# Value loads for two steps at a time, and a value ring that is released and filled by halves, in a graph-attention kernel

## The chip, the cores and the metric

The kernel runs on one core of a Trainium2 chip. The metric is the device time of one launch in microseconds (us). Before the change it is 1956.38 us, the median of three runs (1952.86 to 1957.16).

## What is computed

One graph-attention layer with four heads over 8192 nodes, followed by a residual and a layer norm. Cut to what matters:

```python
Wh = (x @ W.T).reshape(n, 4, 32)                      # n = 8192
score_l, score_r = einsum(Wh, a_l), einsum(Wh, a_r)   # n x 4 each
e = score_l[:, :, None] + score_r.T[None]             # e[n, h, m]
e = where(e >= 0, e, 0.2 * e)                         # leaky relu
e = where((adj + eye > 0)[:, None, :], e, -inf)
out = einsum('nhm,mhd->nhd', softmax(e, axis=2), Wh)  # over m
x = layernorm(x + elu(out))
```

The exponential of a leaky relu has two branches, each of which is a product of a factor of the row and a factor of the column. So the kernel never forms the softmax's matrix. For each node it sums the columns' weighted values twice, over the neighbours with e >= 0 and over the others, and gives each sum its row factor at the end. The two sums are matmuls of 0/1 masks with a table of values.

## The kernel before

**Tiling.** Rows (destination nodes) go in NC = 8 chunks of 1024 (eight sub-tiles of 128), heads in NP = 2 pairs, columns (source nodes) in 32 steps of two tiles of 128. A pass is one chunk c with one pair of heads p; there are 16 passes of 32 steps, 512 steps in all, counted by q. In the text "step 276" is the one with q = 276, and a place in a pass is s = q % 32.

**One step.** ScalarE makes two or three and VectorE one or two of the four 128x1024 comparisons of the step (`bmask`, lines 446 and 591). VectorE ANDs them with the adjacency (`mask_b`, line 603) and XORs the result with the adjacency for the other branch (`mask_c`, line 609). TensorE does 32 matmuls with `bmask`, in some steps turns one pair of adjacency tiles (`turn_pair`, line 315, 16 matmuls), and does 32 matmuls with `cmask` (line 335). ScalarE copies a turned pair from PSUM to `acache` (line 414). `bmask` has four slots and `cmask` two. From step 32 on a pair is turned in every even step.

**Queues.** Every engine's program is written out by hand. SyncE issues every DMA: 396 values per tile and partition from the table `v_scratch` in DRAM into `vring`, the adjacency into the two buffers `abuf` (`load_block`, line 177, 2 MB in two DMAs per four turned tiles), the rows' scores `lrow` (line 186, 1 MB, once a pass), and once a chunk the finished output and the residual's input (`store_y` line 216, `load_xr` line 211, four DMAs of 128 KB each). SyncE takes them strictly in order, so a DMA whose semaphore wait is not met holds up all behind it.

**The ring of values.** `vring` has four slots, one for each step, and `load_v(q)` (line 194) fills slot q % 4. It waits for `mm_done` of q - 3, that is until TensorE has ended step q - 4. The loop issues `load_v(q + 3)` in iteration q, so a load goes out when step q - 1 ends. TensorE waits for `v_in[slot]` at the head of each step.

**Order around the change.** Iteration q of SyncE's loop issues, in this order: the value load, an adjacency block if one is due (in the steady part every fourth iteration, q % 4 == 3), `lrow` at s = 3, and output and residual input at s = 16. The passes of the chunks 1 to 6 are in a hardware loop on TensorE (`pe.Fori(1, NC - 1)`); its program jumps back at the steps 128, 192, 256, 320 and 384.

Of the kernel before, what the change touches and what calls it, by code (L numbers as in the profile page):

```python
# [6 lines left out]
def gat_kernel(nc, x, adj, W, a_l, a_r, out):  # L7
# [10 lines left out]
    NP = 2  # L18
    HP = H // NP
    STEPS = NT // 2  # L20
    Q = NC * NP * STEPS
# [46 lines left out]
    with ctx:  # L68
        def sb(name, shape, dt):
            return ctx.enter_context(nc.sbuf_tensor(name, shape, dt))  # L70

        def sem(name):
            return ctx.enter_context(nc.semaphore(name))

        l_dram = nc.dram_tensor("l_scratch", [NC, H * SUB, P], fp32, kind="Internal").ap()
        v_dram = nc.dram_tensor("v_scratch", [NP, P, NT, VW], bf16, kind="Internal").ap()
# [6 lines left out]
        vring = sb("vring", [P, 4, 2, VW], bf16)  # L83
# [63 lines left out]

        a_loaded = [sem("a_loaded0"), sem("a_loaded1")]
        tr_done, evac_done, pack_made, diag_done = sem("tr_done"), sem("evac_done"), sem("pack_made"), sem("diag_done")
        v_in = [sem(f"v_in{k}") for k in range(4)]  # L150
        lrow_in, cmp_act, cmp_dve = [sem("lrow_in0"), sem("lrow_in1")], sem("cmp_act"), sem("cmp_dve")
        b_ready, c_ready, half_done, mm_done, bank_free = (sem(s) for s in ("b_ready", "c_ready", "half_done", "mm_done", "bank_free"))
        dn_step, w_ready, pool_step, mn_ready, em_ready = (sem(s) for s in ("dn_step", "w_ready", "pool_step", "mn_ready", "em_ready"))
# [5 lines left out]
        def wait(eng, s, value):  # L159

            if not (isinstance(value, int) and value <= 0):
                eng.wait_ge(s, value)
# [8 lines left out]
        def _(sp):  # L171
            def load_block(n):
                c, jb = n // BLOCKS, n % BLOCKS
                wait(sp, tr_done, JB // 2 * (n - 1))
                for half in range(2):
                    rows = adj[c * CI + half * CI // 2:c * CI + (half + 1) * CI // 2, jb * JB * P:(jb + 1) * JB * P]
                    sp.dma_start(abuf[:, n % 2, half * SUB // 2:(half + 1) * SUB // 2],
                                 rows.rearrange("(j p) m -> p j m", p=P)).then_inc(a_loaded[n % 2], 16)

            def load_lrow(c, p):  # L180

                if c > 0:
                    sp.wait_ge(cmp_act, step_no(c - 1, p, STEPS - 1) + 1)
                    sp.wait_ge(cmp_dve, step_no(c - 1, p, STEPS - 1) + 1)
                src = l_dram[c:c + 1, p * HP * SUB:(p + 1) * HP * SUB].rearrange("o i n -> o (i n)").to_broadcast([P, HP * CI])
                sp.dma_start(lrow[:, p].rearrange("q h n -> q (h n)"), src).then_inc(lrow_in[p], 16)

            def load_v(q):
                c, p, s = WHERE[q]
                wait(sp, mm_done, q - 3)  # L190
                if c == 0 and s % EVERY_STEPS == 0:
                    n = p * NG + s // EVERY_STEPS
                    sp.wait_ge(v_out[n % VS], 16 * (n // VS + 1))
                sp.dma_start(vring[:, q % 4], v_dram[p, :, 2 * s:2 * s + 2]).then_inc(v_in[q % 4], 16)

            def store_v(n):

                p, g = n // NG, n % NG
                sp.wait_ge(v_lo, n + 1)
                sp.dma_start(v_dram[p, :, G * g:G * g + G], vt[:, n % VS].rearrange("q t i e -> q t (i e)")).then_inc(v_out[n % VS], 16)  # L200
# [12 lines left out]
            def store_y(c):  # L213
                sp.wait_ge(y_ready, c + 1)
                for s in range(4):
                    sp.dma_start(as_bytes(out, c, s), yout[s::4]).then_inc(y_stored, 16)
# [14 lines left out]
            for g in range(NG):  # L231
                if g in (1, 3, 5, 7):
                    load_block({1: 2, 3: 3, 5: 4, 7: 5}[g])
                store_v(g)
            for q in range(3):
                load_v(q)

            loaded, turned = 6, AHEAD
            for q in range(Q):
                c, p, s = WHERE[q]  # L240
                if q + 3 < Q:
                    load_v(q + 3)
                while loaded < NC * BLOCKS and JB // 2 * (loaded - 1) <= turned:
                    load_block(loaded)
                    loaded += 1
                turned += len(TURNED[q])
                if s == 3 and p == 1 and c < NC - 1:
                    load_lrow(c + 1, 0)
                if s == 3 and p == 0 and c > 0:
                    load_lrow(c, 1)  # L250
                if q < STEPS + 1 and s % EVERY_STEPS == 0 and q > 0:
                    store_v(NG + q // EVERY_STEPS - 1)
                if s == 16 and p == (0 if c else 1):
                    if c > 0:
                        store_y(c - 1)
                    load_xr(c)
# [6 lines left out]
        def _(pe):  # L263
            def settle():
                pe.sem_inc(passed, 1)
# [52 lines left out]
            def step(c, p, u, k, first=False, turned=None):  # L318

                slot, cslot = k % 4, k % 2  # L320
                q = (c * NP + p) * STEPS + 8 * u + k
                w = c * NP + p

                def opens(bank):
                    wait(pe, bank_free, BANKS * (w - 1) + bank + 1)
                    if not isinstance(c, int):
                        settle()

                def product(mask, item, i, h, b, j):
                    bank, at = item // PB, item % PB  # L330
                    opening = first and i == 0 and at == 0
                    if opening:
                        opens(bank)
                    col = (h * 2 + b) * S3
                    return nc.tensor.matmul(psum[:, bank, at * S3:(at + 1) * S3], mask[:, i, j * P:(j + 1) * P],  # L335
                                            vring[:, slot, i, col:col + S3], start=opening, stop=True, skip_group_check=True)

                pe.wait_ge(v_in[slot], 16 * ((c * NP + p) * (STEPS // 4) + 2 * u + k // 4 + 1))
                pe.wait_ge(b_ready, q + 1)
                if not isinstance(q, int):  # L340
                    settle()
                for i in range(2):
                    for h in range(HP):
                        for j in range(SUB):
                            last = product(bmask[:, slot, h], h * SUB + j, i, h, 0, j)
                last.then_inc(half_done, 1)
                if turned:
                    turn_pair(*turned)
                pe.wait_ge(c_ready, q + 1)
                if not isinstance(q, int):  # L350
                    settle()
                for i in range(2):
                    for h in range(HP):
                        for j in range(SUB):
                            last = product(cmask[:, cslot, h], (HP + h) * SUB + j, i, h, 1, j)
                last.then_inc(mm_done, 1)
# [428 lines left out]
```

## Time and profile before

| what | value |
|---|---|
| median of three runs | 1956.38 us |
| the profiled execution | 1956.05 us |
| its span, first to last instruction | 1954.3 us |
| TensorE busy | 1676.7 us (86%) |
| VectorE busy | 1850.1 us (95%) |
| ScalarE busy | 1696.2 us (87%) |
| mean granted TensorE clock | 0.946 |
| value loads | 512 of 198 KB, median 3.4 us from issue to landing |
| adjacency loads | 256 of 1 MB, median 8.0 us |

The matmuls of the steps start from 91 us to 1927 us. The three compute engines are all nearly full, so the busy shares alone do not say which one sets the pace in a stretch; that is read from the waits and from the timeline. Landings of DMAs are read from the DMA view of a window that holds one issue.

### The profile page before, as it was taken

Reading aid. Unit: us, or ns where it says so; the run is one execution under the profiler, and the core shown is the slowest. Engines: PE = TensorE matmul, PEld = TensorE weight load, DVE = VectorE, ACT = ScalarE, POOL = GpSimd, SP = SyncE. Lnnn points to the kernel's source line nnn. Section 1 sums busy time; section 2 is a strip of 40 time slices with the busy share of each in tenths; the row PEclk is TensorE's granted clock in tenths of the full one; section 3 lists DMA queues with packets and bytes.
Section 4 is the critical chain, followed back from the end, with each engine's and each line's share of the span. In section 5 each row is a group of like instructions: output and inputs, shape, how many; then the busy total and the mean of one; then the engine's idle time right before and its main releaser. Section 6 shows DMA issues by size and latency. Waiting matters only on the chain.

```text
span 1954.3 us, 83257 instructions
## 1 busy us (share of the span) xinstructions
PE 1676.7 (86%) x37063; PEld 1650.0 (84%) x37063; DVE 1850.1 (95%) x2056; ACT 1696.2 (87%) x1791; POOL 228.2 (12%) x106
## 2 busy tenths in 40 slices
PE   5188899798978999788988989889898889989894
PEld 5187799797978989788988989789897889989894
DVE  6699999999999999999999999999999999999995
ACT  3599899798988999798989989789897899979892
POOL 1000100401022010211004010220102110040103
PEclk8599999999999999999999999899998999999997
DMA  7899576676666767666766767567675657665221
GB/s 230 313 328 341 194 257 225 202 228 229 209 200 218 255 210 238 202 212 211 236 220 207 236 220 232 193 205 255 207 236 181 227 190 255 230 200 170 60 68 28
DMA packets 240287, 418.06 MB, mean 214 GB/s; under 512 B 14400, under 2 KB 104896, under 8 KB 238016
## 3 DMA queue, kind: packets, MB, share of 16 engines
q1 hardware_dynamic: 240064, 414.83, 64.6%
q8 instruction: 171, 2.80, 0.6%
q14 instruction: 52, 0.43, 0.1%
HBM read 397.48 MB, written 17.30 MB: 212 GB/s over the span
## 4 chain that ended last, share of the span: by engine, by line
ACT 44%; DVE 22%; PE 18%; issue 9%; DMA 5%; POOL 1%; SPq 0%; DVEq 0%; ACTq 0%; POOLq 0%
ACT bmask L446 40%; PE psum L335 15%; DVE bmask L591 7%; DVE bmask L603 5%; DVE cmask L609 5%; ACT acache L414 3%; DMA abuf<-in_adj_dram 3%; DVE acc L615 2%; DMA vring<-v_scratch 2%; PE trp L315 1%; PE psum L280 1%; DMA v_scratch<-vt 1%; DVE st L657 1%; PE psum L289 0%; DVE acache L539 0%
## 5 line engine op out<-in xcount | busy, mean ns | idle before, releaser
L446 ACT ACTIVATE bmask<-lrow,rtab 128x1024 fp8e4<-128x1024 f32 x1450 | 1540.7, 1149 | 11.5 <-PE psum L335 11.5
L335 PE MATMUL psum<-vring,bmask 128*128 128x99 bf16 x16384 | 843.0, 210 | 96.1 <-DVE bmask L603 48.1
L335 PE MATMUL psum<-vring,cmask 128*128 128x99 bf16 x16384 | 844.6, 211 | 89.1 <-DVE cmask L609 80.4
L335 PEld LDWEIGHTS psum<-vring,bmask 128*128 128x128 fp8e4 x16384 | 780.5, 99 | 107.8 <-issue 99.0
L335 PEld LDWEIGHTS psum<-vring,cmask 128*128 128x128 fp8e4 x16384 | 778.5, 99 | 100.5 <-issue 83.4
L603 DVE TENSOR_TENSOR bmask<-bmask,acache 128x1024 int32<-128x1024 int32 x512 | 632.2, 1235 | 41.3 <-ACT bmask L446 32.3
L609 DVE TENSOR_TENSOR cmask<-acache,bmask 128x1024 int32<-128x1024 int32 x512 | 654.7, 1279 | 11.8 <-PE psum L335 11.7
L591 DVE TENSOR_SCALAR bmask<-lrow,rtab 128x1024 fp8e4<-128x1024 f32 x598 | 500.0, 848 | 0.0
L414 ACT CAST acache<-trp 128x512 int32<-128x512 f32 x256 | 148.5, 580 | 167.3 <-PE trp L315 167.0
L720 POOL TENSOR_TENSOR late<-acc,wgt 128x1024 f32<-128x1024 f32 x16 | 45.0, 2810 | 1493.8 <-DVE wgt L645 1493.8
L315 PE MATMUL trp<-pack,abuf 128*128 128x32 bf16 x4096 | 144.1, 177 | 53.7 <-ACT acache L414 32.0
L315 PEld LDWEIGHTS trp<-pack,abuf 128*128 128x128 bf16 x4096 | 128.4, 97 | 56.1 <-issue 32.8
L615 DVE TENSOR_REDUCE acc<-psum 128x165 f32<-128x495 f32 (+1 forms) x112 | 62.7, 621 | 0.8 <-PE psum L335 0.8
L729 POOL TENSOR_SCALAR late<-late 128x512 f32<-128x512 f32 x16 | 36.6, 2289 | 1.4
L419 ACT CAST vt<-acache 128x1056 bf16<-128x1056 f32 x16 | 17.1, 1101 | 17.4 <-DMA v_scratch<-vt 15.8
L743 POOL TENSOR_TENSOR vrs<-mv,epsc 128x8 f32<-128x8 f32 x8 | 7.8, 980 | 191.3 <-DVE mv L661 191.3
L745 POOL TENSOR_TENSOR vrs<-vrs,epsc 128x8 f32<-128x8 f32 x8 | 27.4, 3422 | 0.6
L402 ACT COPY acache<-psum 128x280 f32<-128x280 f32 x32 | 11.0, 395 | 17.9 <-PE psum L280 17.9
L726 POOL TENSOR_TENSOR late<-late 128x512 f32<-128x512 f32 x16 | 25.2, 1576 | 1.3
L453 ACT ACTIVATE late<-late 128x512 f32<-128x512 f32 x16 | 9.9, 617 | 17.4 <-POOL late L729 17.4
L746 POOL TENSOR_TENSOR late<-late,mv 128x1024 f32<-128x1024 f32 x8 | 23.3, 2911 | 0.0
L500 DVE COPY bmask<-psum 128x512 f32<-128x512 f32 x16 | 11.1, 692 | 11.1 <-PE psum L289 11.0
(60 smaller groups left out, 258.5 us busy)
## 6 DMA issues: line engine op xcount, KB each, us to landing
abuf<-in_adj_dram SPq DMA_DIRECT2D x256, 1024.0 KB, 8.0
vring<-v_scratch SPq DMA_DIRECT2D x512, 198.0 KB, 3.4
lrow<-l_scratch SPq DMA_DIRECT2D x16, 1024.0 KB, 10.8
v_scratch<-vt SPq DMA_DIRECT2D x16, 792.0 KB, 9.5
bmask<-in_x_dram SPq DMA_DIRECT2D x16, 256.0 KB, 2.9
late<-in_x_dram SPq DMA_DIRECT2D x32, 128.0 KB, 4.8
out_dram<-late SPq DMA_DIRECT2D x32, 128.0 KB, 6.1
l_scratch<-cmask SPq DMA_DIRECT2D x1, 128.0 KB, 3.7
```

Of the source, the lines that this page charges most:

```text
L315: last = nc.tensor.matmul(trp[:, i, j * P // 4:(j + 1) * P // 4], block_hi, pack[:, :], start=True, stop=True)
L335: return nc.tensor.matmul(psum[:, bank, at * S3:(at + 1) * S3], mask[:, i, j * P:(j + 1) * P], vring[:, slot, i, col:col + S3], start=open ...
L414: nc.scalar.copy(acache[:, at:at + 2].rearrange("p t n -> p (t n)").bitcast(i32), trp.rearrange("p i n -> p (i n)")).then_inc(evac_done, 1)
L446: last = nc.scalar.activation(bmask[:, q % 4, h, i], lrow[:, p, h], ACT.Relu, bias=rtab[:, t, H + hh:H + hh + 1], scale=BIG, saturate=False)
L591: last = nc.vector.tensor_scalar(bmask[:, q % 4, h, i], lrow[:, p, h], rtab[:, t, hh:hh + 1], None, ALU.is_ge, saturate=False)
L603: nc.vector.tensor_tensor(m, m, adj_words(c, s), ALU.bitwise_and).then_inc(b_ready, 1)
L609: nc.vector.tensor_tensor(mask_words(cmask[:, q % 2]), adj_words(c, s), mask_words(bmask[:, q % 4]), ALU.bitwise_xor).then_inc(c_ready, 1)
L615: nc.vector.tensor_reduce(acc[:, b * PB:b * PB + n], psum[:, b, 0:n * S3].rearrange("p (i s e) -> p i e s", s=3, e=E), AX.X, ALU.add).then ...
L720: nc.gpsimd.tensor_tensor(pm[:, :], acc[:, :, 0:DK], wgt.rearrange("p (i o) -> p i o", o=1).to_broadcast([P, ITEMS, DK]), ALU.mult).then_i ...
L726: nc.gpsimd.tensor_tensor(ov[:, :, mine].rearrange("p j (h d) -> p h j d", h=HP), p2[:, 0], p2[:, 1], ALU.add).then_inc(pool_step, 1)
L729: nc.gpsimd.tensor_scalar(mn[:, :, mine], ov[:, :, mine], 0.0, None, ALU.min).then_inc(mn_ready, 1)
L745: nc.gpsimd.tensor_tensor(vrs[:, :], vrs[:, :], epsc[:, SUB:2 * SUB], ALU.pow).then_inc(pool_step, 1)
```

## The change

One DMA now brings the values of two steps (396 KB instead of 198 KB). The four slots are two halves. A load fills a half and waits until both steps that used it are done. `v_in` has two semaphores instead of four; both steps of a half wait for the same value. SyncE issues a load in every odd iteration only.

```diff
-        v_in = [sem(f"v_in{k}") for k in range(4)]
+        v_in = [sem("v_in0"), sem("v_in1")]
...
             def load_v(q):
+
                 c, p, s = WHERE[q]
-                wait(sp, mm_done, q - 3)
+                half = q // 2 % 2
+                wait(sp, mm_done, q - 2)
...
-                sp.dma_start(vring[:, q % 4], v_dram[p, :, 2 * s:2 * s + 2]).then_inc(v_in[q % 4], 16)
+                sp.dma_start(vring[:, 2 * half:2 * half + 2].rearrange("p s i e -> p (s i) e"),
+                             v_dram[p, :, 2 * s:2 * s + 4]).then_inc(v_in[half], 16)
...
-            for q in range(3):
+            for q in (0, 2):
                 load_v(q)
...
-                if q + 3 < Q:
+                if q % 2 == 1 and q + 3 < Q:
                     load_v(q + 3)
...
-                pe.wait_ge(v_in[slot], 16 * ((c * NP + p) * (STEPS // 4) + 2 * u + k // 4 + 1))
+                pe.wait_ge(v_in[slot // 2], 16 * ((c * NP + p) * (STEPS // 4) + 2 * u + k // 4 + 1))
```

On SyncE, around the chunk's output and residual input (s = 16), the kernel before has these rows (`abuf` is adjacency, `vring` values, `out_dram` the output, `late<-in_x_dram` the residual's input):

```order
L194 DMA vring<-v_scratch 128x792 [waits mm_done] x4
L177 DMA abuf<-in_adj_dram 128x4x512 [waits tr_done]
L177 DMA abuf<-in_adj_dram 128x4x512
L194 DMA vring<-v_scratch 128x792 [waits mm_done]
L216 DMA out_dram<-late 32x8x128 [waits y_ready]
L216 DMA out_dram<-late 32x8x128 x3
L211 DMA late<-in_x_dram 32x8x128 [waits y_ready]
L211 DMA late<-in_x_dram 32x8x128 x3
L194 DMA vring<-v_scratch 128x792 [waits mm_done] x3
```

At the same place the changed kernel has these:

```order
L196 DMA vring<-v_scratch 128x1584 [waits mm_done] x2
L177 DMA abuf<-in_adj_dram 128x4x512 [waits tr_done]
L177 DMA abuf<-in_adj_dram 128x4x512
L219 DMA out_dram<-late 32x8x128 [waits y_ready]
L219 DMA out_dram<-late 32x8x128 x3
L214 DMA late<-in_x_dram 32x8x128 [waits y_ready]
L214 DMA late<-in_x_dram 32x8x128 x3
L196 DMA vring<-v_scratch 128x1584 [waits mm_done] x2
```

Four value loads between two adjacency blocks became two. The value load that stood between the adjacency block and the output is now ahead of the block, as the second half of a pair.

Where `lrow` is loaded (s = 3), SyncE before has:

```order
L194 DMA vring<-v_scratch 128x792 [waits mm_done] x4
L177 DMA abuf<-in_adj_dram 128x4x512 [waits tr_done]
L177 DMA abuf<-in_adj_dram 128x4x512
L186 DMA lrow<-l_scratch 128x2048 [waits cmp_dve,cmp_act]
L194 DMA vring<-v_scratch 128x792 [waits mm_done] x4
```

and now:

```order
L196 DMA vring<-v_scratch 128x1584 [waits mm_done] x2
L177 DMA abuf<-in_adj_dram 128x4x512 [waits tr_done]
L177 DMA abuf<-in_adj_dram 128x4x512
L186 DMA lrow<-l_scratch 128x2048 [waits cmp_dve,cmp_act]
L196 DMA vring<-v_scratch 128x1584 [waits mm_done] x2
```

The block and `lrow` stand behind the same iteration's value load as before, and that load's wait is now for one step more.

## Rows read from the trace of the kernel before

**Rows 1.** Page, costliest groups: count, busy us, mean ns, idle before and releaser.
```profile
L446 ACT ACTIVATE bmask<-lrow,rtab 128x1024 fp8e4<-128x1024 f32 x1450 | 1540.7, 1149 | 11.5 <-PE psum L335 11.5
...
L414 ACT CAST acache<-trp 128x512 int32<-128x512 f32 x256 | 148.5, 580 | 167.3 <-PE trp L315 167.0
```
**Rows 2.** Waits: who waited for whom, us in total, times, longest.
```profile
ACT acache L414 <- PE trp L315: 167.0, 73, 8.6
...
PE psum L335 <- DMA vring<-v_scratch: 18.5, 5, 16.9
```
**Rows 3.** Windows: us, busy PE, PEld, DVE, ACT, POOL (instructions), clock, DMA share.
```profile
862.50:895.00 32.50, 32.46 (x769) 32.34 (x766) 31.97 (x34) 32.50 (x35) 0.00 (x0) 1.00 0.78 249
```
**Rows 4.** Timeline of SyncE's queue, 960 to 977 us: start, us, what.
```profile
961.89 2.15 SPq L177 DMA_DIRECT2D abuf<-in_adj_dram  x2
964.39 9.74 SPq L194 DMA_DIRECT2D vring<-v_scratch  x4
```
**Rows 5.** DMA issues in the window 964.3:964.6, last number us to landing.
```profile
vring<-v_scratch SPq DMA_DIRECT2D x1, 198.0 KB, 8.1
```
**Rows 6.** Timeline of TensorE, start of step 244.
```profile
976.48 1.59 PE L335 MATMUL psum<-vring,bmask 128*128 128x99 bf16 x32
```
**Rows 7.** Timeline of SyncE's queue, 1077 to 1099 us.
```profile
1081.11 0.98 SPq L177 DMA_DIRECT2D abuf<-in_adj_dram  x2
1083.61 0.34 SPq L194 DMA_DIRECT2D vring<-v_scratch  x1
1083.99 3.19 SPq L216 DMA_DIRECT2D out_dram<-late  x4
...
1091.21 2.14 SPq L194 DMA_DIRECT2D vring<-v_scratch  x3
```
**Rows 8.** DMA issues in the window 1091.15:1091.5, the load of step 276.
```profile
vring<-v_scratch SPq DMA_DIRECT2D x1, 198.0 KB, 3.8
```
**Rows 9.** Timeline of TensorE, step 276: its start and its turned pair.
```profile
1095.71 1.59 PE L335 MATMUL psum<-vring,bmask 128*128 128x99 bf16 x32
1097.13 0.56 PE L315 MATMUL trp<-pack,abuf 128*128 128x32 bf16 x16
```
**Rows 10.** Timeline of ScalarE: it takes the pair turned in step 276.
```profile
1098.43 0.58 ACT L414 CAST acache<-trp 128x512 int32<-128x512 f32 x1
```
**Rows 11.** DMA totals of the windows 1085:1087 (2048-byte packets) and 1090.4:1092.4 (512-byte).
```profile
DMA packets 380, 0.75 MB, mean 374 GB/s; under 512 B 15, under 2 KB 15, under 8 KB 380
...
DMA packets 1349, 0.66 MB, mean 330 GB/s; under 512 B 82, under 2 KB 1348, under 8 KB 1349
```
**Rows 12.** Timeline of SyncE's queue, 920 to 940 us.
```profile
921.38 2.35 SPq L177 DMA_DIRECT2D abuf<-in_adj_dram  x2
924.13 0.34 SPq L186 DMA_DIRECT2D lrow<-l_scratch  x1
925.40 10.57 SPq L194 DMA_DIRECT2D vring<-v_scratch  x4
```
**Rows 13.** DMA issues in the window 925.3:925.6, the load of step 231.
```profile
vring<-v_scratch SPq DMA_DIRECT2D x1, 198.0 KB, 9.3
```
**Rows 14.** Timeline of TensorE, start of step 232.
```profile
938.32 1.59 PE L335 MATMUL psum<-vring,bmask 128*128 128x99 bf16 x32
```
**Rows 15.** Timeline of TensorE, two idle times of about 2.6 us.
```profile
142.75 0.59 PE L315 MATMUL trp<-pack,abuf 128*128 128x32 bf16 x16 [2.63 <-DMA abuf<-in_adj_dram]
...
693.69 1.60 PE L335 MATMUL psum<-vring,cmask 128*128 128x99 bf16 x32 [2.55 <-DVE cmask L609]
```
**Rows 16.** Windows just after these two idle times; the third number from the end is the clock.
```profile
142.50:145.80 3.30, 3.04 (x48) 3.08 (x49) 2.80 (x3) 2.42 (x3) 0.00 (x0) 0.50 0.99 343
...
693.80:697.00 3.20, 3.03 (x64) 2.80 (x62) 3.20 (x4) 2.76 (x4) 1.10 (x1) 1.00 0.19 45
```
**Rows 17.** Page, DMA queues: packets, MB, share of 16 engines.
```profile
q8 instruction: 171, 2.80, 0.6%
```
**Rows 18.** Timeline of TensorE at the jump back of its loop, step 256.
```profile
1020.83 2.83 PE L335 MATMUL psum<-vring,bmask 128*128 128x99 bf16 x32 [6.69 <-DVE bmask L603]
```

## The prediction

> **What bounds the kernel now.** I read the costliest groups first, then the waits, and then the timeline and the DMA view of a few narrow windows.
>
> The groups give the pace. ScalarE's comparisons and its copies of turned pairs add up to 1540.7 + 148.5 = 1689 us over 512 steps, 3.30 us a step [rows 1]. The steps take 3.6 us on average (91 to 1927 us). ScalarE is idle for 167 us in front of the copy, waiting for TensorE's turned pair [rows 1, 2]. So ScalarE sets the pace wherever TensorE has kept up, and where TensorE is late ScalarE waits for it. In an undisturbed stretch both are full: in 32.5 us ScalarE is busy for 32.50 us and TensorE for 32.46 us [rows 3]. TensorE's lateness of a microsecond or two is therefore not free. It reaches ScalarE as soon as the turned pair comes later than ScalarE gets to it.
>
> The change touches what TensorE waits for at the head of a step. Before, this wait is nearly nothing: 18.5 us in all, 16.9 of them once, before the first step [rows 2]. The reader is to see how little room there is behind that small number.
>
> **What the change does to a load.** Before, the load of step q is issued when step q - 4 ends, with three whole steps to land in. Now the pair (q, q + 1) is issued when step q - 3 ends, and its first step has only two. The adjacency block stands behind a value load in SyncE's queue, so its issue too comes one step later than before. In the steady part the queue is now pair, pair, block. The first pair after a block goes out two steps after it and lands behind it. All of these share one queue, and what I need is how long that queue takes to drain, counted from the block's issue.
>
> *An ordinary place (step 244).* The block is issued at 961.89 and the load of step 243 at 964.39 [rows 4], landing 8.1 us later at 972.5 [rows 5], which is 10.6 us behind the block's issue. The load of 964.39 went out when step 239 ended. Now the pair goes out at that time and the block 0.38 us later (1083.99 - 1083.61, what SyncE needs from one value load to the next DMA [rows 7]), at 964.77. The same bytes and one step's values more are then in the queue. The 198 KB take 0.5 us at 374 GB/s [rows 11]. The pair lands at 964.77 + 10.6 + 0.5 = 975.9. TensorE starts step 244 at 976.48 [rows 6]. It fits with 0.6 us to spare. This is one of the tight ones, since TensorE runs at full pace here. Some ninety places are of this kind and I count them at nothing. At worst, with 0.5 us more in the queue, a few of them are late by tenths.
>
> *Output and residual input (s = 16, p = 0, chunks 1 to 7: seven places, step 276 is one).* Behind the block there is another 1 MB in 512-byte packets. The block is issued at 1081.11 [rows 7] and the load of step 276 lands at 1091.21 + 3.8 = 1095.0 [rows 7, 8], 13.9 us later. TensorE starts step 276 at 1095.71 [rows 9], so before there are 0.7 us to spare. Now the block goes out at 1083.61 + 0.38 = 1083.99. The bytes ahead of the pair are those ahead of the old load, less one step's values that went out earlier. The pair's second step puts them back. So it lands at 1083.99 + 13.9 = 1097.9, and TensorE stands for 2.2 us. The bounds: if SyncE and not the queue sets the landing, its eight issues end 7.2 us after they start [rows 7], at about 1092.2, and with 3.8 + 0.5 us the pair is late by 0.8 us. With 0.5 us more in the queue it is 2.7 us. The DMA engines moved 330 GB/s right before the load's landing [rows 11], so the queue was full and I take 2.2.
>
> How much of this reaches ScalarE? The pair of adjacency tiles turned in step 276 is ready at 1097.13 + 0.56 = 1097.69 [rows 9], and ScalarE, busy until then, takes it at 1098.43 [rows 10]. It hides 0.7 us. 1.5 us are left, times 7 = 10 us (bounds 0 to 14).
>
> *lrow (s = 3, 14 places, step 232 is one).* The block goes out at 921.38, lrow at 924.13, the load of step 231 at 925.40 [rows 12]. That load lands 9.3 us later at 934.7 [rows 13], 13.3 behind the block. Now the block goes out at 925.40 + 0.38 = 925.8, and the pair (232, 233) lands at 925.8 + 13.3 + 0.5 = 939.6. TensorE starts step 232 at 938.32 [rows 14], so it is late by 1.3 us. With ScalarE's 0.7 us hidden 0.6 are left. In the seven places with p = 0, VectorE has the previous chunk's lines 652 and 657 in its queue one and two steps later and is itself the laggard there, so I count nothing. In the seven with p = 1 it is 0.6 x 7 = 4 us. Bounds for all: 0 to 14 x 1.3 = 18 us.
>
> *The clock.* An idle TensorE can be granted 1.2 GHz instead of 2.4 afterwards. Of two idle times of about the same length, one of 2.63 us was followed by a granted clock of 0.50 for 3.3 us, and one of 2.55 us was not (1.00) [rows 15, 16]. The seven stands of 2.2 us are just of this size. A block of 32 matmuls takes 2.83 us at the low clock [rows 18] and 1.60 at the high one [rows 15], and in 3.3 us TensorE falls about 1.4 us behind. ScalarE's slack is by then used up. Half of seven is 3.5 x 1.4 = 5 us (0 to 10).
>
> *The loop's jumps.* At five steps TensorE's program jumps back, and it stands for 6.69 us in the one shown [rows 18]. Programs are read by DMA on a queue of their own, 171 packets of 16 KB in the span [rows 17], on the same DMA engines. The block used to be issued one step before this jump and is now issued at the jump, so such a read meets another load. If it gets ahead of the block, up to all of it could go: 5 x 6.69 = 33 us. If it comes behind the whole block, whose queue takes 10.6 us, it is 5 x (10.6 - 6.7) = 20 us worse. The row nearest is the one of today, with the block already in the queue, so I take a small gain of 0.6 us each, 3 us.
>
> *The first step.* It now waits for 396 KB instead of 198, 0.5 us. SyncE issues 256 DMAs fewer, at 0.32 us each, but it waits for TensorE nearly always; nothing. TensorE has as many waits as before.
>
> *The packets.* They double from 1584 to 3168 bytes. From 512 to 2048 bytes the rate rises from 330 to 374 GB/s, 13% for a factor of four [rows 11]. A pair takes 1.1 us, so even the whole 13% is 0.14 us. Nothing in the sum.
>
> The Trainium skill ("Perfetto Trace Analysis", DMA Optimizations) holds that batching small transfers, for example from 2 KB to 4 or 8 KB, can improve throughput dramatically when a kernel is bound by DMA. By that rule the pairs would land much earlier, the late places would go and the crowded first 24 steps would get faster. The two rates of rows 11 do not bear a dramatic step out in this range of sizes.
>
> **The sum.** 10 + 4 + 5 - 3 + 0.5 = 16.5 us, on the profiled execution's own 1956.05 us (span 1954.3 and 1.75 around it), 0.3 under the median. The forecast is 1972 us. The adjacency blocks have one step less too, but they need not land before the turn four steps later, some 14 us after their issue against about 10 us of queue.
>
> **The rivals.**
>
> 1. *Everything lands on the path, and more: 1997 us.* No slack in ScalarE, every late place counted whole: 7 x 2.2 + 14 x 1.3 = 34 us, with the low clock at each of the seven, 10 us, less 3 for the jumps. For it speaks that ScalarE is never idle in the 32.5 us of rows 3. Against it speaks the slack of rows 10.
>
> 2. *The late pairs are hidden: 1956 us.* The queue drains faster since no single value loads stand in it, or TensorE's start in these places is late for other reasons. It needs landings 2 us earlier at the seven places. Against it speak the full DMA engines.
>
> 3. *Faster, by the jumps: 1943 us.* The place is the head of a pass, steps 128 to 384. The program's read finds an empty queue since the block is issued behind it. It decides from about 17 us on, half of the 33: the price is 1956 + 20 (without my 3) - 33 = 1943. For it speaks that the block is today in the queue when the jump comes and will not be. Against it: the block follows 0.4 us after the jump.
>
> 4. *Batching pays: 1966 us.* With packets a fixed 13% cheaper, a pair is 0.14 us earlier. At 21 places this is 3 us, and the first 24 steps gain 12 pairs x 0.14 = 2 us. It changes the size and not the sign. The page's rule named above is this rival; so far as the rows go it is worth 5 us and no more.
>
> **How the numbers follow.** The forecast with its own range 1962 to 1984 has 0.66, the fourth rival 0.04 within it, rival 1 0.12, rival 2 0.10, rival 3 0.08. Faster by over 0.2% (4 us, about what a measurement of this kernel can tell from no change) comes from rival 3: 0.08. No change is rival 2: 0.10. Slower has the rest, 0.82. The range 1957 to 1990 leaves out rival 3, most of rival 2 and the worst of rival 1.
>
> **What the profile of the changed kernel would show.** In the waits, TensorE's wait for `vring` grows from 18.5 us to 40 to 60 us, in about 21 pieces besides the first, at s = 20 of the passes with p = 0 (about 2 us each) and at s = 8 of nearly all (about 1 us each). ScalarE's 167 us for the turned pair grow by 12 to 20 us. A landing of a pair two steps behind a block takes 4 to 5 us, and 7 to 8 us with lrow or the output in the queue. Idle before step 256 a little under 6.7 us. The prediction is wrong if these pieces are there and the time is not longer, if the pairs at s = 20 land before TensorE comes, or if the gaps at the jumps change by more than 2 us each.

## The result, and the profile after

The changed kernel takes 1992.9 us, median of four runs (1987.91 to 1997.71), against 1956.77 us. The ratio is 1.0189, with a 95% interval of 1.016 to 1.0217. Repeated in a later call it is 1.0194 (1.0163 to 1.0224). The change costs about 37 us. The direction was the forecast one, and the size was more than twice the forecast's 16.5 us and outside its range. Single runs of the kernel before spread from 1938.6 to 1968.5 us over all calls (three slow runs of 3.3 to 8.3 ms, one each of three kernels, are left out of all ratios), so a place in one trace is read to a microsecond only where a mechanism stands behind it.

The page's first part and the lines that answer to [rows 1], of the changed kernel (its lines stand three further down than before):

```profile
span 1991.8 us, 83001 instructions
...
PE 1692.0 (85%) x37063; PEld 1665.0 (84%) x37063; DVE 1850.4 (93%) x2056; ACT 1699.1 (85%) x1791; POOL 227.5 (11%) x106
...
L449 ACT ACTIVATE bmask<-lrow,rtab 128x1024 fp8e4<-128x1024 f32 x1450 | 1539.0, 1144 | 13.7 <-PE psum L338 13.7
...
L417 ACT CAST acache<-trp 128x512 int32<-128x512 f32 x256 | 148.2, 579 | 199.1 <-PE trp L318 198.8
```

No engine has more instructions to do. TensorE's busy time grew all the same, from 1676.7 to 1692.0 us, for its 37063 matmuls, as its mean granted clock went from 0.946 to 0.941. ScalarE's work is the same to 2 us, and its idle time in front of the copy of a turned pair has grown from 167 to 199 us. The 32 us are most of the 37.5 us between the two spans: ScalarE waits for a TensorE that is late. Why TensorE is late is in the waits of the changed kernel (us in total, times, longest), where [rows 2] has 18.5 us for the values:

```profile
PE psum L338 <- DMA vring<-v_scratch: 45.4, 19, 16.4
PE psum L338 <- DVE acc L618: 38.6, 40, 4.0
...
PE psum L338 <- issue: 27.6, 31, 3.4
PE trp L318 <- issue: 19.9, 6, 5.1
```

The wait for values grew by 27 us. The last two lines are idle times of TensorE that no semaphore explains; together they were 19.2 us before and are 47.5 us now. Part of this growth is a name only: 21.6 us of the 47.5 stand at the loop's five jumps, and there the kernel before has about 32 us of idle time that the trace puts down to VectorE ([rows 18] is one of the five). Elsewhere this idle time grew from 19 to 26 us.

**Behind the output (step 276).** The changed kernel's timeline of SyncE's queue and of TensorE, and the landing of the pair (DMA issues, window 1120.2:1120.6), to be set beside [rows 7 to 9]:

```profile
1110.15 0.34 SPq L196 DMA_DIRECT2D vring<-v_scratch  x1
1110.53 1.48 SPq L177 DMA_DIRECT2D abuf<-in_adj_dram  x2
1112.05 3.45 SPq L219 DMA_DIRECT2D out_dram<-late  x4
1115.55 4.69 SPq L214 DMA_DIRECT2D late<-in_x_dram  x4
1120.28 0.60 SPq L196 DMA_DIRECT2D vring<-v_scratch  x1
```

```profile
vring<-v_scratch SPq DMA_DIRECT2D x1, 396.0 KB, 4.2
```

```profile
1120.80 1.60 PE L338 MATMUL psum<-vring,cmask 128*128 128x99 bf16 x32
1124.71 1.59 PE L338 MATMUL psum<-vring,bmask 128*128 128x99 bf16 x32 [2.31 <-DMA vring<-v_scratch]
1126.14 0.56 PE L318 MATMUL trp<-pack,abuf 128*128 128x32 bf16 x16
```

The pair lands at 1120.28 + 4.2 = 1124.5, which is 13.95 us behind the block's issue. The forecast had 13.9, and an idle time of 2.2 us; it is 2.31. SyncE needs 8.2 us for the eight issues, so the pair goes out about 4 us after its release (step 273 ended at about 1116.3). In ScalarE's timeline the turned pair now has to be waited for:

```profile
1126.73 0.59 ACT L417 CAST acache<-trp 128x512 int32<-128x512 f32 x1 [1.68 <-PE trp L318]
```

1.68 us against the forecast's 1.5. The same idle time of 1.7 to 2.8 us stands at all seven such places.

**Behind lrow (step 232).** In the changed kernel TensorE waits 1.19 us for the pair, against the 1.3 forecast from [rows 12 to 14]:

```profile
964.05 1.59 PE L338 MATMUL psum<-vring,bmask 128*128 128x99 bf16 x32 [1.19 <-DMA vring<-v_scratch]
```

Its twin at step 296 is put down to another releaser:

```profile
1196.82 1.59 PE L338 MATMUL psum<-vring,bmask 128*128 128x99 bf16 x32 [1.28 <-DVE bmask L606]
```

The pair and not VectorE was the last to come there: the block was issued at 1182.85 and the pair landed 13.7 us later, at 1196.5, just before TensorE started. So the sum of the vring line above is short by such places.

**At the jump (step 256).** The idle time of 6.69 us [rows 18] became two, and the second lies in the middle of the turned pair:

```profile
1043.33 2.15 PE L338 MATMUL psum<-vring,bmask 128*128 128x99 bf16 x32 [3.71 <-DVE acc L618]
...
1050.70 0.48 PE L318 MATMUL trp<-pack,abuf 128*128 128x32 bf16 x11 [5.09 <-issue]
...
1062.58 1.60 PE L338 MATMUL psum<-vring,cmask 128*128 128x99 bf16 x32 [0.80 <-DVE cmask L612]
```

The last line is TensorE's wait for VectorE in step 259. In the kernel before it is 1.8 us longer:

```profile
1036.80 2.83 PE L335 MATMUL psum<-vring,cmask 128*128 128x99 bf16 x32 [2.56 <-DVE cmask L609]
```

VectorE sets the pace at the head of a pass (it is busy for 15.10 of the 15.20 us from 1020.8 to 1036 in the kernel before), and TensorE's longer stand is hidden behind it. From step 252 to step 260 the kernel before takes 37.7 us and the changed one 36.8. Over all five jumps these eight steps take 187.6 us before and 185.5 us now (185.3 in the second trace of the changed kernel). So the jumps cost the changed kernel nothing: they give back 2 us.

**The clock.** After the late pair of step 276 the clock stayed at its upper level, and after the one of step 340 it was at the lower (windows; the third number from the end is the clock):

```profile
1124.70:1128.00 3.30, 3.29 (x81) 3.30 (x82) 2.99 (x4) 1.62 (x3) 0.00 (x0) 1.00 0.99 309
1358.40:1361.70 3.30, 3.30 (x54) 3.30 (x52) 3.17 (x5) 1.40 (x2) 0.00 (x0) 0.50 0.98 314
```

It fell at four of the seven places.

### The profile page after: what moved, and what is told of

It reads as the page before. It is cut to its first block, busy times and chain, and to the rows that moved or that the text cites. A ratio compares the mean times of both kernels' runs of the same rounds, so it can differ in the third digit from the quotient of the medians.

```text
span 1991.8 us, 83001 instructions
## 1 busy us (share of the span) xinstructions
PE 1692.0 (85%) x37063; PEld 1665.0 (84%) x37063; DVE 1850.4 (93%) x2056; ACT 1699.1 (85%) x1791; POOL 227.5 (11%) x106
## 4 chain that ended last, share of the span: by engine, by line
ACT 36%; PE 25%; DVE 19%; issue 9%; DMA 7%; SPq 2%; POOL 1%; DVEq 0%; ACTq 0%; POOLq 0%
ACT bmask L449 33%; PE psum L338 22%; DVE bmask L594 6%; DVE bmask L606 5%; DMA vring<-v_scratch 4%; DVE cmask L612 4%; ACT acache L417 2%; DMA abuf<-in_adj_dram 2%; PE trp L318 2%; DVE acc L618 2%; SPq L214 1%; DMA v_scratch<-vt 1%; PE psum L283 1%; SPq L219 1%; DVE st L660 1%
## 5 line engine op out<-in xcount | busy, mean ns | idle before, releaser
L449 ACT ACTIVATE bmask<-lrow,rtab 128x1024 fp8e4<-128x1024 f32 x1450 | 1539.0, 1144 | 13.7 <-PE psum L338 13.7
L338 PE MATMUL psum<-vring,bmask 128*128 128x99 bf16 x16384 | 851.8, 211 | 113.8 <-DMA vring<-v_scratch 45.4
L338 PEld LDWEIGHTS psum<-vring,bmask 128*128 128x128 fp8e4 x16384 | 788.4, 99 | 127.4 <-issue 117.9
L612 DVE TENSOR_TENSOR cmask<-acache,bmask 128x1024 int32<-128x1024 int32 x512 | 646.0, 1262 | 29.0 <-PE psum L338 28.4
L740 POOL TENSOR_TENSOR late<-late 128x1024 f32<-128x1024 f32 x8 | 22.7, 2840 | 0.6
```

Source lines behind the costliest of these rows:

```text
L449: last = nc.scalar.activation(bmask[:, q % 4, h, i], lrow[:, p, h], ACT.Relu, bias=rtab[:, t, H + hh:H + hh + 1], scale=BIG, saturate=False)
L612: nc.vector.tensor_tensor(mask_words(cmask[:, q % 2]), adj_words(c, s), mask_words(bmask[:, q % 4]), ALU.bitwise_xor).then_inc(c_ready, 1)
```

## The experiments

Theory A says that pairs of values land late behind a block with something else in the queue. Rival B says that the block's new time disturbs the reads of TensorE's program. Rival C says that the larger DMA is itself the cost. All ratios are against runs of the kernel before on the same chip; a difference of two ratios from different calls is one between two chips.

### Eight slots, all issue times kept

```diff
-        vring = sb("vring", [P, 4, 2, VW], bf16)
+        vring = sb("vring", [P, 8, 2, VW], bf16)
...
-                wait(sp, mm_done, q - 2)
+                wait(sp, mm_done, q - 4)
...
-                if q % 2 == 1 and q + 3 < Q:
-                    load_v(q + 3)
+                if q % 2 == 1 and q + 5 < Q:
+                    load_v(q + 5)
```

This is cut, and set against the changed kernel. `v_in` has four semaphores for the four halves, and `w_nat` and `w_t` lie in `acc` to make room.

> The changed kernel with eight slots (four halves): every DMA of SyncE goes out at the same time as in the changed kernel, but a pair of values is for two steps later, so its first step has four steps to land in and not two. w_nat and w_t share memory with acc. Theory A (pairs of values that land after TensorE has come, behind the adjacency block and lrow or the output): all these idle times go, about 34 us of the 36, and what is left is the start of the kernel, where blocks are waited for; 1959 to 1968 us, wait for vring only before the first step. Rival B (the blocks' later issue disturbs the reads of TensorE's program): nothing of that is changed here, so 1980 us or more.

Measured: 1.0065 (1.0041 to 1.009). The waits of this kernel:

```profile
PE psum L338 <- issue: 39.5, 34, 3.5
PE psum L338 <- DVE acc L618: 34.7, 40, 3.7
...
PE psum L338 <- DMA vring<-v_scratch: 16.3, 1, 16.3
PE trp L318 <- issue: 15.6, 7, 3.6
```

The wait for values is the one before the first step. Giving the pairs room takes 1.25% (24 us) off. What stays is 0.65%, more than the few microseconds of the start, and the idle time that no semaphore explains is 55 us, 21 of them at the five jumps. So theory A has two thirds of the loss, and something else has a third.

### Two single loads, released as the pair is

```diff
-                wait(sp, mm_done, q - 3)
+                wait(sp, mm_done, q - 2 - q % 2)
-                if q + 3 < Q:
+                if q % 2 == 1 and q + 3 < Q:
                     load_v(q + 3)
+                    load_v(q + 4)
```

> The kernel before, with its single loads of 198 KB and four semaphores, but both loads of a pair are issued together when the second of the two old steps has ended, as the changed kernel does. Theory A (the lateness of the release, not the size of the DMA): the same as the changed kernel within 5 us, 1988 to 1998 us; SyncE's second issue costs 0.3 us and the first step's values land 0.5 us earlier, so if anything 1 to 4 us less. Rival C (one DMA of 396 KB with 3168-byte packets is itself the cost): near the kernel before, 1956 to 1965 us.

Measured: 1.0269 (1.0231 to 1.0307), 0.8% worse than the pair. Rival C falls; the expectation of 1 to 4 us less was wrong in sign. SyncE's queue and TensorE at step 296, and that load's landing (window 1200.2:1200.3):

```profile
1193.71 0.80 SPq L194 DMA_DIRECT2D vring<-v_scratch  x2
1194.55 0.98 SPq L177 DMA_DIRECT2D abuf<-in_adj_dram  x2
1195.63 0.45 SPq L186 DMA_DIRECT2D lrow<-l_scratch  x1
1200.24 0.81 SPq L194 DMA_DIRECT2D vring<-v_scratch  x2
...
1209.03 1.15 PE L336 MATMUL psum<-vring,bmask 128*128 128x99 bf16 x22 [2.69 <-DMA vring<-v_scratch]
```

```profile
vring<-v_scratch SPq DMA_DIRECT2D x1, 198.0 KB, 8.5
```

The step's values land 14.2 us behind the block's issue (13.7 with the pair), and the block itself goes out 0.46 us later, because SyncE issues two loads before it. The idle time is 2.69 us where the pair has 1.28. With the release as it now is, one DMA is better than two. Why by 0.8% is open in part: of the 15 us between the two traces' spans 8 lie in steps 24 to 64, and no run looks into them.

### The block one step later in the kernel before

```diff
                 while loaded < NC * BLOCKS and JB // 2 * (loaded - 1) <= turned:
+                    if q > 32:
+                        wait(sp, mm_done, q + 1)
                     load_block(loaded)
```

> The kernel before with one thing more: from step 33 on SyncE issues an adjacency block only when the step of that iteration has ended, one step later, as in the changed kernel. Value loads behind it in SyncE's queue are then due at once and go out at nearly the same time as before. Theory A: nothing waits for the block, and value loads land up to 1 us later than before with up to 1 us of room; 1956 to 1964 us. Rival B (the block's new place disturbs the reads of TensorE's program): 1966 us or more, with more idle time in front of TensorE that no semaphore explains, at the jumps and inside the passes.

Measured: 1.0279 (1.024 to 1.0319). Its waits:

```profile
PE psum L337 <- DMA vring<-v_scratch: 75.6, 42, 16.2
...
PE trp L317 <- issue: 14.8, 5, 4.0
...
PE psum L337 <- issue: 13.8, 20, 1.9
```

The number would fit rival B, and the first line says otherwise; the unexplained idle time is 29 us, 9 more than before, and cannot hold 55 us. The load of step q % 4 == 3 goes out at its old time and now has the block directly in front of it, not one step earlier. Most of the loss is behind lrow: the 14 steps with s = 7 have 42 of the 59 us of waits behind the first one. At step 231, one of them, the block goes out at 951.26 and the load at 952.79, which lands 11.1 us later at 963.9, 12.6 us behind the block, and TensorE starts at 964.08. I had allowed it 1 us of lateness. The run tells of the queue and says little of program reads. It also suggests why the changed kernel does not lose more: its two values of a pair stand ahead of the block.

### lrow at s = 5

```diff
-                if s == 3 and p == 1 and c < NC - 1:
+                if s == 5 and p == 1 and c < NC - 1:
-                if s == 3 and p == 0 and c > 0:
+                if s == 5 and p == 0 and c > 0:
```

> The changed kernel with lrow issued at s = 5 of a pass and not at s = 3, so that no adjacency block is in front of it and no pair of values directly behind both. Theory A, as the profile after has it (the 14 late pairs at s = 8 pass on almost whole, 1.2 us each): 15 to 19 us less, 1974 to 1978 us, and the waits for vring at s = 8 are gone. The forecast's own reckoning (0.6 us at seven of them and nothing at the others): 4 us less, 1989 us.

Measured: 1.0192 (1.0157 to 1.0228), no gain. The late pairs at s = 8 are gone, and two steps later stands this (TensorE's timeline, step 234):

```profile
963.41 0.88 PE L338 MATMUL psum<-vring,bmask 128*128 128x99 bf16 x16
966.21 0.88 PE L338 MATMUL psum<-vring,bmask 128*128 128x99 bf16 x16 [1.91 <-issue]
```

In the DMA view of 962 to 967 us a program packet starts while the data queue is full:

```profile
q1 hardware_dynamic: 907, 1.89, 100.2%
q8 instruction: 1, 0.02, 1.1%
```

TensorE stops between two matmuls of one block of 32, where it waits for no semaphore. Theory A's 15 to 19 us less did not come; a gain of 4 us, the forecast's, would be within the noise. That moving 1 MB by two steps only changed what it was in the way of fits this place. But the unexplained idle time of the whole run, 50 us, is only 2 us above the changed kernel's, so a gain that was taken back is not shown.

### Output and residual input at s = 18

```diff
-                if s == 16 and p == (0 if c else 1):
+                if s == 18 and p == (0 if c else 1):
```

> The changed kernel with the output and the residual's input issued at s = 18 and not at s = 16, behind a pair of values two steps after the adjacency block and no longer directly behind the block. Theory A (late pairs at s = 20 pass on almost whole, with the low clock at about half of them; the profile after shows 19 us over s = 12 to 32 of the seven passes): 14 to 22 us less than the changed kernel if nothing else is hit, ratio to before about 1.009 to 1.012. Rival D (the same bytes hit something else there, as lrow did when it was moved, a read of TensorE's program): a ratio of 1.016 to 1.020.

Measured: 1.0089 (1.0057 to 1.0121), and in the next call but one 1.0106 (1.0076 to 1.0135). SyncE's queue and TensorE around step 276:

```profile
1094.48 0.98 SPq L177 DMA_DIRECT2D abuf<-in_adj_dram  x2
1100.25 0.34 SPq L196 DMA_DIRECT2D vring<-v_scratch  x1
1100.63 2.64 SPq L219 DMA_DIRECT2D out_dram<-late  x4
...
1106.19 1.59 PE L338 MATMUL psum<-vring,bmask 128*128 128x99 bf16 x32
```

The pair goes out 5.8 us behind the block, ahead of the output, and TensorE does not stand. Seven places are worth about 0.9%, 18 us. Theory A holds for them, and rival D falls.

### Eight slots, the block at its old time

```diff
-                if q % 2 == 1 and q + 5 < Q:
-                    load_v(q + 5)
+                if q % 2 == 0 and q + 4 < Q:
+                    load_v(q + 4)
...
+                    wait(sp, mm_done, q)
                     load_block(loaded)
```

> Merged loads alone: one DMA for two steps into eight slots, issued when step q - 1 of even iterations q ends, for the steps q + 4 and q + 5, so a pair has four steps to land in, and an adjacency block goes out when the same step ends as in the kernel before (one step earlier than in the changed kernel and in the run with eight slots). Theory A with the part of rival B that the first runs left (4 us of program reads at s = 10 come from the block's later issue): ratio to before 0.996 to 1.002, no waits for vring behind the first step, and idle time in front of TensorE at s = 10 of the passes with p = 1 back to about 0.5 us each. If merging itself costs (rival C), 1.005 or more.

Measured: 0.9983 (0.9959 to 1.0008), 0.8% less than the first run with eight slots. Its waits:

```profile
PE psum L339 <- issue: 20.3, 21, 6.0
...
PE trp L319 <- issue: 5.8, 4, 2.2
```

26 us of unexplained idle time where the other kernel with eight slots has 55. The jumps are not in the difference: with every name counted, TensorE stands there for 31.8 us in all with the late block and 31.5 with the early one. Away from them it is 34 us against 14. At step 170, TensorE's timeline of that one and then of this one:

```profile
723.08 0.78 PE L338 MATMUL psum<-vring,bmask 128*128 128x99 bf16 x14 [1.80 <-issue]
```

```profile
720.86 0.78 PE L339 MATMUL psum<-vring,bmask 128*128 128x99 bf16 x14 [0.44 <-issue]
```

The two kernels differ only in when the block and the pairs go out, so that order costs 0.8%, 16 us (9 to 23 by the two intervals), more than I thought. Both times moved in this run: the block's by one step, and the pairs' from the odd to the even iterations. No run separates the two. The two traces, of single executions on two chips, are only 8 us apart.

That the idle time is a read of TensorE's program held up by the data queue is argued. For it speaks a 16 KB program packet in the DMA view around step 170 of the first kernel, beside a data queue at 102.6%, where the second has a queue at 53.8%. For it speaks too where these times stand. A pass of TensorE's program is eight steps written out and then a loop over eight steps that runs three times (`pe.Fori(1, 4)` in `one_pass`); this loop is missing in the description of the order around the change. In the passes of the chunks 1 to 6 every idle time above 0.3 us without a semaphore, in all fifteen traces, stands at s = 0 to 15, while a part of the program runs for the first time in its pass, and none in the repeats from s = 16 on. No run took the reads away, so the cause is not shown.

### The block ahead of the values in the first 24 steps

```diff
+                if q < 24 and loaded < NC * BLOCKS and JB // 2 * (loaded - 1) <= turned:
+                    load_block(loaded)
+                    loaded += 1
                 if q % 2 == 0 and q + 4 < Q:
```

> The same as the run with eight slots and the block's old place, and in the first 24 steps the adjacency block goes out ahead of the pair of values, as soon as its buffer is turned and not when the step ends. Theory A on the start of the kernel (there TensorE waits for the block's landing, and the change put 198 KB more in front of it): steps 0 to 24 get shorter by 5 to 15 us against the kernel before, ratio 0.990 to 0.997. If the start is bound by the bytes that the DMA engines can move and not by the order: no difference to the run without it.

Measured: 0.993 (0.9903 to 0.9957). At a median of 1941.13 us it is the fastest version of the study. Step 24 starts at 190.7 us in the trace of before, at 197.3 us in that of the changed kernel, at 192.7 us in the run without this edit and at 185.0 us here. TensorE's timeline here, and this kernel's wait for blocks, which was 15.5 us before and is 14.7 us in the changed kernel:

```profile
184.99 1.59 PE L342 MATMUL psum<-vring,bmask 128*128 128x99 bf16 x32
```

```profile
PE trp L322 <- DMA abuf<-in_adj_dram: 4.4, 3, 2.7
```

So in the start TensorE waits for blocks, and what stands ahead of a block in the queue, and when it is let go, is paid there: 8 us between these two traces. The edit changes both at once and does not tell them apart. This part of theory A holds.

### Both moves, on the changed kernel, the kernel before and the fastest one

```diff
-                if s == 3 and p == 1 and c < NC - 1:
+                if s == 25 and p == 1 and c < NC - 1:
...
-                if s == 16 and p == (0 if c else 1):
+                if s == 18 and p == (0 if c else 1):
```

The first pair of lines moves lrow, and the line for p == 0 is changed alike; the second moves the output and the residual's input. First the changed kernel once more, unchanged:

> The changed kernel once more, beside the three others of this call: ratio to before 1.016 to 1.022 by every theory.

Measured: 1.0194 (1.0163 to 1.0224). The changed kernel with both moves:

> The changed kernel, four slots, with the output and the residual's input at s = 18 and lrow at s = 25, where no block is in front of it and TensorE's program is not being read for a new loop. Theory A with lrow's share of the program reads: no late pairs at s = 8 and s = 20, what is left is the start (4 us, blocks behind two steps' values) and 2 to 6 us of program reads; ratio 1.000 to 1.005. If lrow moved here hits something else as it did at s = 5: 1.009 or more.

Measured: 1.0088 (1.0061 to 1.0114), above the 1.000 to 1.005 expected of theory A and close to the 1.009 of lrow hitting something else. Its profiled run, 1957.84 us, is 13 us faster than its other four, so no place is read from its trace alone. The kernel before with both moves:

> The kernel before with the same two moves and nothing else. If they only remove what the change made late, the kernel before has nothing to gain from them: ratio 0.998 to 1.001. If lrow beside a block also slows the program reads of the kernel before (0.5 to 2 us of idle time at s = 8 to 13): 0.993 to 0.998.

Measured: 1.0004 (0.9981 to 1.0026). The kernel before gains nothing from the moves, so what they gave the changed kernel is what the change had made late. The fastest version with both moves:

> Eight slots, block's old place, block ahead of the values in the first 24 steps, and both moves: the gains of the start (8 us) and of the moves together; ratio 0.986 to 0.992. If the moves have nothing to give where no pair is late: the same as without them, 0.993.

Measured: 0.9943 (0.9921 to 0.9966), the same as without them. Where no pair is late they give nothing. That lrow also slows program reads elsewhere found no support in these two runs.

### lrow's share, measured on one chip

The output's move alone, with the edit shown above for it:

> The changed kernel with the output and the residual's input at s = 18 once more, beside the kernel that also moves lrow, so that their difference is measured on one chip. Ratio 1.006 to 1.012.

Measured: 1.0106 (1.0076 to 1.0135). Both moves:

> Both moved once more. If the 14 late pairs behind lrow cost what the profile after shows of them (7 to 9 us over s = 4 to 12 and s = 36 to 44 beyond what the run with eight slots has there), 0.3 to 0.5% less than the run beside it. If they are hidden, as the forecast had most of them: within 0.1% of it.

Measured: 1.0061 (1.0033 to 1.0088), 0.45% less than the run beside it. Over both calls the output's move alone has 1.0098 and both have 1.0075. lrow's late pairs cost 0.2%, some 4.5 us, with the two calls giving 0 and 9. The size stays open between these.

## Why the prediction was wrong

The steps of the sum, against ratios of the runs. One per cent is 19.5 us. A measured step is the difference of two ratios, mostly from different chips, and is sure to some 7 us.

| step | forecast | measured |
|---|---|---|
| pairs behind the output, with the clock | 10 + 5 = 15 us | 1.0191 to 1.0098: 18 us |
| pairs behind lrow | 4 us | 1.0098 to 1.0075: 4.5 us (0 to 9) |
| other late pairs | 0 | 1.0075 to 1.0065: 2 us, within the noise |
| the block and the pairs one step later (jumps, first step) | -3 + 0.5 us | 1.0065 to 0.9983: 16 us (9 to 23) |
| one DMA for two steps, with eight slots | 0 | 0.9983: -3 us (-8 to 2) |

The traces say where. These are differences of step starts in TensorE's timeline, in us against the trace of before. The two traces of the changed kernel differ by up to 3 us in a row.

| stretch | changed kernel, two traces | eight slots, late block | eight slots, early block |
|---|---|---|---|
| steps 0 to 24 (99.3 before) | +6.4, +8.0 | +4.5 | +2.2 |
| eight steps around each of the five jumps (187.6) | -2.1, -2.3 | -1.1 | +1.4 |
| s = 4 to 16 of the twelve passes of chunks 1 to 6 (503.0) | +13.3, +14.2 | +4.5 | -9.9 |
| s = 16 to 32 of the seven passes with the output (353.7) | +17.0, +19.7 | +0.5 | +0.6 |

**The late pairs** were right in mechanism, place and nearly in number. The idle time is 2.3 us behind the output (2.2 forecast) and 1.2 us behind lrow (1.3). The landing behind a block could be carried over from the kernel before to 0.1 us at step 276. At the ordinary places nearly nothing is late, as forecast. The share that ScalarE hides (0.7 us) and the low clock at half of the seven (four of seven) held too. The term behind the output came out 3 us short, and all late pairs together 5: forecast 19 us, measured 24.

**The step that failed** is the price of everything that goes out one step later and is not a late pair: -3 us for the jumps, "0.5 us" for the first step, and nothing else. The runs have 16 us (9 to 23) in its place. Its part on the jumps, "so I take a small gain of 0.6 us each, 3 us", came out in size, 2 us by the traces, but not by its argument, which was luck: the first idle time at step 256 shrank from 6.69 to 3.71 us and not by a little, a second of 5.09 us appeared, and the longer sum did not count since VectorE sets the pace there. By the forecast's own sign of being wrong (a gap at a jump changed by more than 2 us) it had the jump wrong.

What it put at nothing, without a reason, are two other places. The start of the kernel: steps 0 to 24 take 6 to 8 us longer in the changed kernel, where one step's values were written off as 0.5 us once and nothing was counted for the blocks behind them. And the stretch s = 4 to 16 inside the passes, which takes 14 us longer with the late block than with the early one, both with eight slots and no late pair (+4.5 against -9.9 us; against the kernel before only the 4.5 are a loss). Traces spread here: without late pairs, the three with the late block have 503 to 512 us in this stretch and the five with the early one, the kernel before among them, 493 to 503. There TensorE stops in the middle of a block of matmuls, at step 170 for 1.80 us with the late block and for 0.44 us with the early one. The forecast looked for program reads at the outer loop's five jumps alone. That these stops are program reads stays argued, and how the 16 us divide between the block's time and the pairs' stays open.

**The rivals.** That all is hidden fell, as did a gain by the jumps that outweighs the rest. Rival 1 (1997 us) had the time nearly right, and for the wrong reason: it put the excess on late pairs that are not hidden, and the eight-slot run leaves 0.65% with no late pair at all. (The fourth rival's price should read 1967 us, 5 under the forecast.) The fourth rival's rule from the Trainium skill ("Perfetto Trace Analysis", DMA Optimizations), that batching small transfers can lift throughput dramatically, has its own run: merging with eight slots and the block at its old time gives 0.2%, with an interval that includes nothing. The rule is for kernels bound by DMA, and the data queue took 64.6% of the DMA engines' time before, so this run shows how little it has to give here and does not refute it. In the release order of the change the merged load was 0.8% better than two single ones, which is not dramatic either.

**What it should have looked for in the profile.** The wait for values grew to 45 us and the waits behind lrow and the output came as described (19 pieces, some under another name). ScalarE's wait for the turned pair grew by 32 us where 12 to 20 were forecast. That line holds most of what was missed: it says how much reaches the end, whatever the reason. An idle time without a semaphore does not: those at the jumps are long and cost nothing. The time of a fixed number of steps, before and after, settles which of them count.

## What to carry to other kernels

When a load is merged and its release moves, list every other DMA that stands behind it in the issuing queue; here the adjacency block, itself untouched, was issued one step later, and that new order of block and pairs cost up to 16 us beside the 24 us of all late values. Count a load's room from the issue of the largest transfer ahead of it and not from its own issue. If a ring of four is to be released by halves, give it more slots: with eight (six were not tried), the block at its old time and ahead of the values in the start, the merged loads ran at 0.993 of the kernel before.

## What was unexpected of the hardware

- TensorE can stop inside a row of 32 equal matmuls where it waits for no semaphore: 1.91 us at step 234 of the run with lrow at s = 5, with a 16 KB program packet beside a full data queue. A trace shows this as idle time by "issue". In the passes of the chunks 1 to 6 it happened only in the first sixteen steps, where the program's parts run for the first time, and not in the repeats of the loop behind them.
- Two DMAs of 198 KB can land later than one of 396 KB. At step 296 the first of the two came 14.2 us behind the block's issue and the pair 13.7 us, with the same bytes ahead.
- The same four issues of SyncE can take very different times. Those of the residual's input took 4.69 us at s = 16, where they start 5.0 us behind the block's issue, and 2.62 us at s = 18, 8.8 us behind it. The DMA engines were full in both (share 1.05 and 1.01), so a busy engine alone does not stretch them:

```profile
1103.32 2.62 SPq L214 DMA_DIRECT2D late<-in_x_dram  x4
```

- An idle time of TensorE of 1.7 to 2.8 us was followed by the lower clock at four of seven places. Its length alone does not tell which: 1.93 us was, 2.31 us was not.
